# Residual additions of an attention stage moved from VectorE to GpSimd, with statistics and roots later

## The reference, cut to what matters

```python
x = x + _L0_xattn_ref(_layernorm(x), ctx_1024, ctx_1024, 0, mask_SxS2_ff0)

xq = q.reshape(b, s, 8, 4, 16)       # q: the normed x, 32 heads of 16
xk = k.reshape(b, t, 8, 16)          # k and v: the context, 8 groups of 16
scores = jnp.einsum('bsgrd,btgd->bgrst', xq, xk) / math.sqrt(16) + mask
probs = jax.nn.softmax(scores, axis=-1)
out = jnp.einsum('bgrst,btgd->bsgrd', probs, xv)
```

## Time and profile before

| what | value |
|---|---|
| median of 3 runs | 1158.39 us (1158.16 to 1161.39) |
| the profiled execution | 1158.27 us, its span 1156.3 us |
| TensorE, VectorE, ScalarE, GpSimd busy | 94%, 58%, 43%, 32% of the span |
| the second attention in the trace | from about 200 us to 349 us |

### The profile page before, as it was taken

How to read it: one execution, slowest core, us unless ns; L and a number is a source line. 1 busy time by engine, 2 the same in 40 slices (tenths; PEclk the granted TensorE clock), 3 DMA queues, 4 the chain that set the end, 5 groups by cost and what they waited for, 6 DMA issues and landing times.

```text
span 1156.3 us, 24200 instructions
## 1 busy us (share of the span) xinstructions
PE 1087.6 (94%) x9586; PEld 568.4 (49%) x9586; DVE 666.5 (58%) x1212; ACT 499.7 (43%) x986; POOL 375.7 (32%) x339
## 2 busy tenths in 40 slices
PE   7889998999998989999999999999979999999996
PEld 3445454676664444444444444444446544444442
DVE  7768785799987755335214412522268824646465
ACT  4566773888855634322111211211269822322231
POOL 2345574766723310000560160000044400606073
PEclk9988999999998999999999999999989999999998
DMA  7000000111300202210120010000000000000000
GB/s 249 2 3 4 19 16 16 53 49 46 96 4 25 89 23 83 78 56 1 41 63 0 0 54 0 1 1 1 1 10 13 2 1 1 27 9 27 9 37 37
DMA packets 29661, 36.01 MB, mean 31 GB/s; under 512 B 6530, under 2 KB 21147, under 8 KB 29436
## 3 DMA queue, kind: packets, MB, share of 16 engines
q1 hardware_dynamic: 28154, 34.60, 9.5%
q10 hardware_dynamic: 1410, 0.06, 0.1%
HBM read 30.24 MB, written 4.19 MB: 30 GB/s over the span
## 4 chain that ended last, share of the span: by engine, by line
PE 68%; DVE 8%; ACT 3%; POOL 3%; issue 2%; POOLq 0%; DVEq 0%; ACTq 0%
PE p_up L116 10%; PE p_up L117 10%; PE p_up L118 10%; PE p_y L116 9%; PE p_y L118 9%; PE p_y L117 9%; PE p_up L110 2%; DVE wf_lo L246 2%; PE p_y L2435 1%; PE p_up L2402 1%; PE p_y L2430 1%; PE p_y L2423 1%; PE p_y L1562 1%; POOL wd_lo L1315 1%; ACT wd_hi L2357 1%
## 5 line engine op out<-in xcount | busy, mean ns | idle before, releaser
L1989 DVE TENSOR_TENSOR d_h_low<-d_hf,d_h_high 128x512 f16<-128x512 f32 (+1 forms) x40 | 27.9, 697 | 204.9 <-ACT d_h_high L2078 204.9
L116 PE MATMUL p_up<-d_xt_high,wd_hi 128*128 128x512 f16 (+1 forms) x352 | 134.2, 381 | 2.9 <-PE p_y L118 1.5
L117 PE MATMUL p_up<-d_xt_low,wd_hi 128*128 128x512 f16 (+1 forms) x352 | 134.2, 381 | 0.0
L118 PE MATMUL p_up<-d_xt_high,wd_lo 128*128 128x512 f16 (+1 forms) x352 | 133.9, 381 | 0.0
L170 ACT ACTIVATE d_sg<-p_up 128x512 f32<-128x512 f32 (+1 forms) x40 | 23.8, 594 | 212.8 <-PE p_up L118 212.7
L116 PE MATMUL p_y<-wd_hi,d_h_high 128*128 128x512 f16 (+1 forms) x272 | 103.1, 379 | 0.0
L118 PE MATMUL p_y<-wd_hi,d_h_low 128*128 128x512 f16 (+1 forms) x272 | 103.1, 379 | 0.0
L117 PE MATMUL p_y<-wd_lo,d_h_high 128*128 128x512 f16 (+1 forms) x272 | 103.1, 379 | 0.0
L138 POOL TENSOR_SCALAR wd_raw<-wd_raw 128x1156 f32<-128x1156 f32 x8 | 25.1, 3138 | 208.8 <-DVE d_h_low L1989 208.8
L438 POOL TENSOR_TENSOR a_pt_low<-a_ex,a_pt_high 128x1024 f16<-128x1024 f32 x32 | 68.3, 2133 | 71.8 <-ACT a_pt_high L930 71.6
L2259 POOL TENSOR_TENSOR wd_hi<-wd_hi,e_den 128x1024 f32<-128x1024 f32 x16 | 30.5, 1908 | 136.8 <-DVE e_den L2295 136.8
(11 more groups left out here) (341 smaller groups left out, 2757.9 us busy)
## 6 DMA issues: line engine op xcount, KB each, us to landing
wd_raw<-in_w_d SPq DMA_DIRECT2D x16, 616.0 KB, 3.7
wd_raw<-in_w_f SPq DMA_DIRECT2D x8, 578.0 KB, 3.8
X<-in_x SPq DMA_DIRECT2D x4, 1024.0 KB, 12.2
wd_lo<-in_ctx_t SPq DMA_DIRECT2D x128, 32.0 KB
out_x<-wd_raw SPq DMA_DIRECT2D x16, 256.0 KB, 2.0
wd_lo<-in_ctx SPq DMA_DIRECT2D x32, 64.0 KB, 2.4
wd_raw<-in_w_c SPq DMA_DIRECT2D x1, 1096.0 KB, 12.4
wd_hi<-in_Wo SPq DMA_DIRECT2D x1, 1024.0 KB
```

The source lines that it names most:

```text
L116: nc.tensor.matmul(ps, st[0], mv[0], start=start, stop=False)
L117: nc.tensor.matmul(ps, st[0], mv[1], start=False, stop=False)
L118: return nc.tensor.matmul(ps, st[1], mv[0], start=False, stop=stop)
L1989: nc.vector.tensor_tensor(hid[1][0:n, d % NH, :], value, hid[0][0:n, d % NH, :], ALU.subtract).then_inc(h_ready, 1)
```

## The change

The additions of tiles 0 to 11 (`own` = 12) go from VectorE to GpSimd. GpSimd does `add(t - 4)` as the last step of its key work for tile t, for t from 4 to 15, after a wait for its own last instruction and for `z_ready` (both units of the tile written to `o`). Tiles 12 to 15 are added by VectorE as before, with a semaphore of their own (`x_last`). Since another engine now reads `o`, `norm_o` of every tile from the third on waits until the tile two before has been added. `measure` comes one tile, that is two units, later: `measure(n // 2 - 3)` at even n, and two measures stand behind the loop in place of one. The roots of a chunk come after the second tile of the chunk after next, so after tiles 9 and 13, and the last two sets behind the loop; before, they came after tiles 7, 11 and 15 and once behind the loop.

```diff
@@ gpsimd, tile(c, i, fresh) @@
                                                 vb[0][r, part, :, h, 0:DH], ALU.subtract).then_inc(vb_ready, 1)
+                    if t >= TC:
+                        add(t - TC, made + VB)
+
+                def add(t, values_done):
+                    pool.wait_ge(vb_ready, values_done)
+                    wait_apart(pool, z_ready, 2 * t + 2, held.apart)
+                    nc.gpsimd.tensor_tensor(held.X[:, t, :], held.X[:, t, :],
+                                            o[:, t % 2, :, :, :, :].rearrange("p k q h d -> p (k q h d)"),
+                                            ALU.add).then_inc(x_ready, 1)
...
                 for c in range(1, NC):
                     for i in range(TC):
                         tile(c, i, True)
-                    rstd_next(c - 1)
+                        if c >= 2 and i == 1:
+                            rstd_next(c - 2)
+                rstd_next(NC - 2)
                 rstd_next(NC - 1)
@@ vector @@
+                def added(t):
+
+                    if t < own:
+                        v.wait_ge(x_ready, t + 1)
+                    else:
+                        v.wait_ge(x_last, t - own + 1)
...
                     v.wait_ge(rec_ready, n + 1)
+                    if t >= 2:
+                        added(t - 2)
                     nc.vector.tensor_tensor(
...
-                    if n >= 2 and n % 2:
+                    if n % 2 and n // 2 - 1 >= own:
                         add(n // 2 - 1)
...
-                    if n >= 4 and n % 2 == 0:
-                        measure(n // 2 - 2)
+                    if n >= 6 and n % 2 == 0:
+                        measure(n // 2 - 3)
+                measure(NT - 2)
                 measure(NT - 1)
```

More of the change, by code:

```diff
@@ L1254, in part_b @@
             s_ready, top_ready, sub_ready, exp_ready, t_ready, pt_high, pt_ready, v_ready, rec_ready, \
-            z_ready, x_ready, bn_ready, stats, nm_ready = (sem(n) for n in (
+            z_ready, x_ready, x_last, bn_ready, stats, nm_ready = (sem(n) for n in (
                 "vb_ready", "xn_ready", "tr_ready", "hi_ready",
                 "xt_ready", "bd_high", "bd_ready", "ks_ready", "s_ready", "top_ready", "sub_ready", "exp_ready", "t_ready",
-                "pt_high", "pt_ready", "v_ready", "rec_ready", "z_ready", "x_ready", "bn_ready", "stats", "nm_ready"))
+                "pt_high", "pt_ready", "v_ready", "rec_ready", "z_ready", "x_ready", "x_last", "bn_ready", "stats", "nm_ready"))
+        own = NT - TC
         kt_in = [sem(f"kt_in_{b}") for b in range(2)]
@@ L1400, in add @@
                                             o[:, t % 2, :, :, :, :].rearrange("p k q h d -> p (k q h d)"),
-                                            ALU.add).then_inc(x_ready, 1)
+                                            ALU.add).then_inc(x_last, 1)
                 def measure(t):
-                    v.wait_ge(x_ready, t + 1)
+                    added(t)
                     nc.vector.bn_stats(held.st[:, t % TC, :], held.X[:, t, :]).then_inc(bn_ready, 1)
```

## The result

| | before | changed |
|---|---|---|
| median of 7 runs each | 1158.82 us (1158.16 to 1161.78) | 1166.51 us (1163.28 to 1169.79) |
| ratio | | 1.0071, 95% interval 1.0045 to 1.0097 |
| the profiled execution | 1158.27 us, span 1156.3 | 1165.87 us, span 1163.8 |
| its mean granted clock | 0.980 | 0.975 |

A forecast was written before the change was run, and what follows sets the result against it. The second attention was taken as bound by a loop over VectorE, TensorE and ScalarE, not VectorE's load. 0 + 1.7 + 2.1 + 0.5 + 0.9 = 5.2 us on 1158.27 gave 1163.5 us, range 1160.0 to 1168.0.

The forecast's parts named there:

- additions off VectorE, tiles without roots: Second attention: twelve 0.75 us additions leave VectorE but only lengthen idle time; ten tiles without roots wait for nothing: 0.
- second wait on `norm_o`: A satisfied second wait ahead of `norm_o`'s product on VectorE costs 0.07 us each, 28 times: 1.7 us, bounds 0 and 2.0.
- lateness behind tiles 9 and 13, with `norm_o` one tile later: Roots behind GpSimd's addition delay ScalarE 1.06 us at each place (2.1); `norm_o` then waits 0.25 us, twice (0.5).
- tail: Behind the loop, one more pair of statistics on VectorE delays `low_z(0)` and TensorE's `turn_z(0)`: 0.9 us on the path.
- the clock at the end of the stage: From 349 to 357 us TensorE's clock is partly low; 0.9 us more waiting may lengthen that part by a us.
- What bounds the stage: Second attention: a loop over VectorE, TensorE and ScalarE sets odd iterations; VectorE's list is just as long in even ones.
- Rival 3: VectorE bounds the second attention after all, so 12 x 0.75 = 9.0 us comes off: 1151 us; chance 0.05.
- the change takes nothing from this list: VectorE's even-iteration list, as long as the loop, keeps its work; its statistics only become one tile older.
- rival 2: GpSimd becomes the bound: an addition of 1.71 us makes `norm_o` wait; 8.6 us, 1166.9 us; decides from 1.44 us; chance 0.15.
- The slack of 0.17 us at `norm_o`: At tiles without roots GpSimd's addition ends at 239.73 and `norm_o` needs it at 239.90, so nothing waits.
- 268.05: Predicted end of GpSimd's addition one tile after roots, against `norm_o` at 267.82: a wait of about 0.25 us.
- Rival 1: Paid but small: the second wait is free and half the delay at the roots is absorbed; 2 us, 1160.3 us; chance 0.30.

The follow-up runs named there:

- e7: Kernel before without the residual additions of tiles 0 to 11 (VectorE only sends the signal): 1157.18 us, ratio to before 1.0006.
- e8: Changed kernel with roots split into GpSimd's gaps at tiles 10, 11, 14, 15 and tile 12's statistics one unit earlier: 1156.80 us, before 1156.92.
- e1: Changed kernel, but VectorE also adds tiles 5 and 9, so no addition precedes the roots behind tiles 9 and 13: 1160.92 us, before 1159.42.
- e5: Kernel before with one more, long satisfied wait ahead of `norm_o`'s product on VectorE, 28 times: 1158.97 us, before 1156.92.
- e6: Changed kernel with eight unread 512-column matmuls on TensorE ahead of attend in iterations 17 and 25: 1161.95 us, before 1159.42.
- e9: Kernel before with one more power of 128x4 in the roots behind tiles 7 and 11, result overwritten: 1163.73 us, before 1158.94.
- e2: Changed kernel with the roots split between GpSimd's two subtractions of tiles 10, 11, 14 and 15: 1158.99 us, before 1159.42.
- e3: Changed kernel with the statistics of tile 12 one unit earlier, so one pair stands behind the loop: 1165.33 us, before 1159.42.
- e10: The changed kernel run once again, with nothing altered: one run, 1164.71 us.
- e4: Kernel before with the roots of its first two chunks between the subtractions of tiles 8 and 12: 1158.66 us, before 1156.92.

## Why the prediction came out right, and where it did not

Forecast 1163.5 us, range 1160.0 to 1168.0, chance for slower 0.60; measured 1166.51. The sum was 5.2 us, the stage became 6.03 us longer, and that these are so close is in part luck: 2.7 us of clock were missing, and against them stand 1.7 us for a wait that costs nothing and 1.0 us for tiles that got shorter.

| term | forecast, us | in the traces |
|---|---|---|
| additions off VectorE, tiles without roots | 0 | -1.0 |
| second wait on `norm_o` | 1.7 | 0 |
| lateness behind tiles 9 and 13, with `norm_o` one tile later | 2.1 + 0.5 | 2.6 |
| the clock behind them | none | 2.7 |
| tail | 0.9 | 0.95 |
| the clock at the end of the stage | "may lengthen that part by a us", in the range only | 0.8 |

- **What bounds the stage** was right. Rival 3 is dead by e7: without the additions at all the loop gains 1.45 us, not 9. The zero for the removed additions was a little low: the loop outside of the two places with roots is 70.35 us (111.42 - 20.58 - 20.49) after 71.37 (107.16 - 17.90 - 17.89). Of this 1.0 us, 0.4 is the one slow tile of before; the other 0.6 is real, 0.08 us in each undisturbed tile, and e7 has it with nothing but the additions gone. So the step "the change takes nothing from this list" of the even iteration failed: it is 4.46 us now, where it was 4.49 to 4.58 before. Which instruction gives the 0.08 us was not isolated.
- **The price of the addition** (1.27 us), of its gap (0.20 for 0.25) and the casts (0.87) were right, and so rival 2, which needed 1.44 us, did not come. Of the Trainium skill's page "GPSIMD Engine Reference" the collision in the section "Specifications" agrees with the casts at 0.87 us instead of 1.22; the advice in "Engine selection" against elementwise additions on GpSimd is not borne out as a cost at tiles where GpSimd has room (e8), and is where it has none (e1 against the changed kernel). The slack of 0.17 us at `norm_o`, read from one tile, did not hold at all ten tiles: at one of them it waits 0.27 us.
- **The second wait** is the step that failed outright. The pair L614 and L618 of the first attention differs by 0.08 us (0.38 and 0.46), but not because of a second wait as such: `norm_o` starts 0.28 us after its reciprocal with it and without it (232.54, and e5). What does make the pair of the first attention slower stays open. In its code the second wait stands ahead of the one for the reciprocal, in `norm_o` behind it; no run here swaps them.
- **The places with roots** were right in mechanism and size as far as the forecast went: 2.1 and 0.5 make 2.6 us, and e6, where the clock stays up, shows 2.58 (1.28 + 1.30). The second term is seen only there (waits of 0.39 and 0.30 us one tile later): in the changed kernel VectorE itself is so late behind the low clock that `norm_o` waits for no addition at these places. (The forecast's 268.05 adds up to 268.03, which changes nothing.) What the sum lacked is that TensorE, when it stands dry for 1.76 us instead of 0.65, is granted the lower clock behind it: 2.70 us more (1.40 + 1.30), by e6 against the changed kernel. e9 shows it without the change.
- **The tail** had the size but not the make-up. While the clock stays up (e1, e2) it is 0.97 us longer: 0.29 because `norm_o` waits for an addition (at 335.47 in the changed kernel), the rest for the late statistics. But the forecast read that TensorE's "list has nothing else before" `turn_z(0)`, and that is wrong. Ahead of it stand twelve matmuls of 128x512. In before they start 0.22 us apart and the last is done when `low_z(0)` is, at about 349.0:

```profile
348.61 0.38 PE L117 MATMUL p_y<-wd_hi,d_term 128*128 128x512 f16 x1
348.83 0.38 PE L118 MATMUL p_y<-wd_hi,d_term 128*128 128x512 f16 x1
```

In the changed kernel the clock falls near the end of the tail, the first eight of them start 0.43 us apart, and `turn_z(0)` follows them without idle time, 0.97 us after the end of `low_z(0)` (355.76):

```profile
355.06 0.63 PE L116 MATMUL p_y<-wd_hi,d_term 128*128 128x512 f16 x1
355.49 0.55 PE L117 MATMUL p_y<-wd_hi,d_term 128*128 128x512 f16 x1
...
356.73 0.22 PE L1831 MATMUL p_y<-c_ident_h,c_zcat 128*96 128x128 f16 x1
```

```profile
353.00:355.00 2.00, 2.00 (x6) 0.68 (x5) 1.88 (x6) 0.00 (x0) 0.11 (x1) 0.50 0.00 0
...
357.00:359.00 2.00, 0.38 (x1) 0.10 (x1) 1.11 (x4) 0.86 (x2) 1.37 (x6) 1.00 0.00 0
```

So the end of the stage is 1.77 us late (0.95 + 0.82), TensorE's list sets it, and the second pair of statistics is hidden behind that list; e3 shows it by taking the pair away for no gain. The clock term was right in size by luck: the forecast had the low stretch that before has behind the update grow longer, and what came is another one, ahead of `low_z(0)`.

Why it falls there stays open. TensorE stands 1.49 us idle in before, in the changed kernel and in e2 alike, and only in the changed one does the clock fall right behind it. It fell in all five traces with late roots (the changed kernel, e3, e6, e9, e10), in e7, which has none, and in none of the other six (before, e1, e2, e4, e5, e8).

- **The total.** 6.03 us of the profiled executions' 7.6 are the stage, 1.54 are scatter ahead of it. Rival 1 (2 us) was right that the second wait is free, and wrong in that half of the delay at the roots would be absorbed: none of it was, and it was doubled. Of the signs that the forecast named, ScalarE's wait at the two places, the prices of addition and casts came as said (the idle time of VectorE was 1.27 us for 1.1 to 1.2); the 0.07 us at `norm_o` and the longer tile period did not come, and `turn_z(0)` was later by 1.77 us, not 0.9.

## What to carry over

When work is moved to an engine that is busy for 5 of 8 us, look for the few places where that engine has a second job behind the moved one, and price those; the other ten places were free but for one wait of 0.27 us. Where such a delay lets TensorE run dry for a time that it did not before, look at the granted clock in the windows behind: here it cost as much as the delay. Before calling a new step at the end of a list "on the path", read to the last row what the engine that waits for it does until then. Work that nobody waits for soon (the roots) belongs in a gap in which its engine waits anyway; there the same four instructions cost nothing.

## What the runs showed of the hardware

- A pause of 1.71 to 1.78 us in a TensorE that is busy for 7.6 us and more of most windows of 8 us ahead of it was followed by the lower clock eight times out of eight (changed kernel, e3, e9, e10, twice each); windows of 8 and 13 us that hold the fall show a mean of 0.79 to 0.87, the first of the changed kernel 0.95 and 0.84, since the fall is spread over two. Behind the pause of 0.65 us in the kernel before it stayed at 1.00. Eight matmuls of 128x512 in the pause (1.90 us) kept it at 1.00 both times. Behind a pause of 1.48 to 1.49 us at the end of the stage it fell in six traces and stayed up in six.
- At the lower clock eight transposes of 128x128 f32 took 1.72 us for 1.09, two matmuls of 128x512 bf16 1.06 us for 0.59, and matmuls of 128x512 f16 in a row started 0.43 us apart for 0.22.
- Two casts of 64x256 f32 to f16 on GpSimd took 1.15 to 1.33 us in before at nearly all tiles where VectorE made the addition, and 0.87 or 0.88 at tiles where it did not (e7, the changed kernel). In e1, where VectorE makes the additions of tiles 5 and 9 alone, just the casts beside them take 1.23 us. The other way round, the additions beside the casts take 0.79 us, the others 0.69.
- A wait that has long been reached is free on VectorE ahead of an instruction that waits for another semaphore anyway, when it stands behind that other wait: 0.28 us with and without (e5).
- On GpSimd an addition of 128x512 f32 from and to SBUF took 1.27 us (12 of them, 1268 ns on average), and did not slow VectorE's instructions, which read PSUM for one input beside it. A power of 128x4 takes 1.04 us, nearly as much.
